# Writing out the small unit loops and dropping the increments behind the waits in a fused convolution and attention kernel

## The reference

```python
# layer 0: kernels turned by an angle that the input gives, grouped 3x3 convolution, gate
rot = vmap(vmap(_rotate_one, (None, 0)))(base_kernel, angles)
feat = conv(x, rot, feature_group_count=B * G)
return feat * sigmoid(relu(pooled @ meta_w1.T + meta_b1) @ meta_w2.T + meta_b2)
# layer 1: focused linear attention
q = (relu(q) + 1e-06) / scale ; k = (relu(k) + 1e-06) / scale
q = q**3 / norm(q**3) * norm(q) ; k = k**3 / norm(k**3) * norm(k)
kv_state = einsum('bjc,bjd->bcd', k, v)
z = 1.0 / (einsum('bic,bc->bi', q, k.sum(axis=1)) + 1e-06)
out = einsum('bic,bcd->bid', q, kv_state) * z
out = out + depthwise_5x5(v)
return out @ Wproj.T + bproj
# together
x = x + layer0(group_norm(x)) ; x = x + layer1(group_norm(x))
```

## Time and profile before

| | us |
|---|---|
| median of 3 timed executions | 3786.84 |
| lowest, highest | 3786.37, 3790.71 |
| profiled execution | 3783.43 |
| its span in the trace | 3781.6 |

### The profile page before, as it was taken

The page is one execution under the profiler, slowest core; times in us unless marked ns, Lnnn a source line. Parts: engine busy times, 40 slices in busy tenths (PEclk is TensorE's granted clock), DMA queues, the critical chain, the costliest instruction groups (busy, mean ns, idle before and its releaser), DMA issues.

```text
span 3781.6 us, 84370 instructions
## 1 busy us (share of the span) xinstructions
PE 3485.4 (92%) x27988; PEld 2840.5 (75%) x27988; DVE 2762.7 (73%) x6715; ACT 2658.7 (70%) x7096; POOL 1606.0 (42%) x1557
## 2 busy tenths in 40 slices
PE   1669999999999999999999999999999999999897
PEld 1238787877878778787877878787787878778786
DVE  7776876767787676777767677776767777575747
ACT  2347777777777777777867777776777777676775
POOL 5542553625345262544626254462625436250402
PEclk9889999999999999999999999999999999999999
DMA  6662634536354453635445363544626343360402
GB/s 222 207 194 68 188 114 143 156 108 190 104 171 118 142 170 97 192 113 161 122 141 176 92 191 120 150 130 124 196 80 192 118 148 113 109 181 1 119 6 79
DMA packets 559906, 515.10 MB, mean 136 GB/s; under 512 B 97600, under 2 KB 491968, under 8 KB 559552
## 3 DMA queue, kind: packets, MB, share of 16 engines
q1 hardware_dynamic: 555200, 508.99, 44.7%
q10 hardware_dynamic: 4352, 1.57, 0.2%
HBM read 351.06 MB, written 134.22 MB: 128 GB/s over the span
## 4 chain that ended last, share of the span: by engine, by line
PE 76%; DVE 10%; ACT 8%; issue 4%; DMA 1%; SPq 1%; POOL 0%; DVEq 0%; ACTq 0%; POOLq 0%
PE SM L1524 15%; PE F L1541 15%; PE VAB L1541 8%; PE PP L1632 7%; PE F L1580 6%; PE VAB L1580 6%; PE T L1552 5%; PE VAB L1610 5%; PE T L1601 3%; PE F L1543 2%; ACT K L1308 2%; PE T L1620 2%; PE VAB L1543 1%; DVE F L996 1%; DVE XR L1068 1%
## 5 line engine op out<-in xcount | busy, mean ns | idle before, releaser
L1541 PE MATMUL F<-WQ,XHL 128*128 128x256 f16 x6144 | 812.7, 273 | 15.9 <-ACT V L1345 15.9
L661 POOL TENSOR_TENSOR XR<-XR,V 128x512 f32<-128x512 f32 x256 | 325.8, 1273 | 904.3 <-DVE XR L1057 904.3
L1314 ACT ACTIVATE K<-K,SCAL 128x256 f32<-128x256 f32 x1024 | 514.0, 509 | 225.4 <-DVE K L1002 224.6
L636 POOL TENSOR_TENSOR SL<-PL,SL 128x1122 f16<-128x1122 f32 x112 | 259.9, 2320 | 970.5 <-DVE SL L970 970.5
L1541 PEld LDWEIGHTS F<-WQ,XHL 128*128 128x128 f16 (+1 forms) x6144 | 599.9, 98 | 89.6 <-issue 19.8
L1524 PE MATMUL SM<-SL,BD 128*128 128x512 f16 x2688 | 634.9, 385 | 0.0
L1308 ACT ACTIVATE K<-F,SCAL 128x256 f32<-128x256 f32 x1024 | 474.8, 469 | 215.3 <-DVE F L996 213.3
L1002 DVE TENSOR_TENSOR K<-K,F 128x512 f32<-128x512 f32 x512 | 350.4, 684 | 228.8 <-PE T L1552 112.3
L1524 PEld LDWEIGHTS SM<-SL,BD 128*128 128x128 f16 x2688 | 260.9, 97 | 284.2
L996 DVE TENSOR_TENSOR F<-F,FL 128x512 f32<-128x512 f32 x512 | 353.5, 690 | 144.5 <-PE F L1543 139.5
L1632 PE MATMUL PP<-XR,WP 128*128 128x256 f16 x3072 | 380.6, 274 | 46.1 <-DVE XR L1075 46.1
(11 more groups left out here) (202 smaller groups left out, 6864.1 us busy)
## 6 DMA issues: line engine op xcount, KB each, us to landing
XR<-xr SPq DMA_DIRECT2D x132, 512.0 KB, 5.0
U<-x SPq DMA_DIRECT2D x256, 256.0 KB, 3.4
XR<-x SPq DMA_DIRECT2D x256, 256.0 KB, 4.1
out<-XR SPq DMA_DIRECT2D x256, 256.0 KB, 3.4
PL<-xp SPq DMA_DIRECT2D x112, 561.0 KB, 3.8
RX<-xr SPq DMA_DIRECT2D x118, 512.0 KB, 3.8
x<-RX SPq DMA_DIRECT2D x448, 128.0 KB, 2.8
BD<-RX SPq DMA_DIRECT2D x240, 96.0 KB, 2.2
```

Source lines behind the costliest of these rows:

```text
L661: g_.tensor_tensor(o, o, fm, ALU.add).then_inc(o_rdy, 2)
L1314: a.activation(K2[:, p, t * C:(t + 1) * C], K3[:, p, t * C:(t + 1) * C], ACT.Square, scale=inv_a, accum_out=S6[:, 2 * p + t:2 * p + t + 1] ...
L1541: t_.matmul(o, XHL[:, xa, h, at], WQ[:, wa, h, c0:c0 + C], start=(k == 0), stop=False)
```

## The change

All `carry(...)` calls, the function and the semaphore go. A wait that had one is then taken up by the operation that follows it: with one wait the operation itself waits; with several, the first one written goes onto the operation and the later ones onto event instructions ahead of it. The loops on VectorE, TensorE and ScalarE become Python loops, so that their rounds are written out with constants. Instructions in the program, before and after: TensorE 24781 and 27612, VectorE 8362 and 8665, ScalarE 4095 and 5633, GpSimd 3209 and 2112, SyncE 2995 and 2007. No computing instruction changes its place among the others on any engine. The lines of the new program are 35 to 45 lower (L1308 is L1266, L1541 is L1499, L661 is L623).

The core of the diff:

```diff
-        carried = sem("carried")
...
-        def carry(eng):
-            eng.sem_inc(carried, 1)
...
                 ins.then_inc(rot_chain, 1)
                 pool.wait_ge(rot_chain, c * N_ROT + steps[0])
-                carry(pool)
...
             def add_depthwise(b, u, p):
                 m = b * PAIRS + 2 * u + p
                 pool.wait_ge(z_rdy, 4 * m + 4 + Z_CR)
-                carry(pool)
...
             def batch(b, ahead):
                 s1, s2, s3 = ahead >= 1, ahead >= 2, ahead >= 3
                 low_v(b, 0, 0)
-                with dve.Fori(1, 5) as u:
+                for u in range(1, 5):
                     for p in range(2):
                         step_kv(b, u, p)
...
-                with act.Fori(1, NU) as u:
+                for u in range(1, NU):
                     for p in range(2):
                         step_kv(b, u, p)
...
                 pe.wait_ge(ones_rdy, b + 1)
-                carry(pe)
-                with pe.Fori(1, 5) as u:
+                for u in range(1, 5):
                     for p in range(2):
                         step_kv(b, u, p)
...
                 pe.wait_ge(fm_rdy, HD * (b + 1) + FM_CR)
-                carry(pe)
                 pe.wait_ge(state_rdy, 4 * HPH * (b + 1))
                 if s2:
 
                     if s3:
                         pe.wait_ge(zb_rdy, b + 4)
                     pe.wait_ge(root_rdy, b + 5)
                     pe.wait_ge(wt_in, 256 * (b + 3))
-                    carry(pe)
```

More of the change, by code:

```diff
@@ L346, in load_taps @@
                     sp.wait_ge(tp_rdy, i - 2)
-                    carry(sp)
                 sp.dma_start(taps_tile(i), toeplitz[:, i * PIX:(i + 1) * PIX]).then_inc(taps_in[i % 3], 16)
@@ L858, in deviations @@
                 dve.wait_ge(s0_rdy, pixels)
-                carry(dve)
                 if not early(k):
                     dve.wait_ge(s1_rdy, results)
-                    carry(dve)
                 for layer in range(2):
```

## The result

| | before | after |
|---|---|---|
| median | 3787.49 us (4 runs, 3786.37 to 3790.71) | 3919.03 us (4 runs, 3918.45 to 3920.87) |
| ratio, with 95% interval | | 1.0348 [1.0335, 1.0361] |
| span of the profiled execution | 3781.6 us | 3917.3 us |

The account below looks back on a forecast made before the run. TensorE, busy 92% of the span, was taken to bound the kernel, with VectorE at 73%. Terms of -2, -1.3, -1.8, -3.9, -0.9 and -0.6 summed to -10.5 us, from 3786.84 to 3776.3, range 3765 to 3790.

Parts of the forecast that it names:

- What bounds the kernel: Whole kernel: TensorE busy 92%, VectorE 73%; only setup, batch 14's query phase and a handful of gaps can be shortened.
- Part 1, the loops: Writing out loops: -0.6 us at TensorE's loop entry, -1.3 from ScalarE's loop at the key/value phase's end.
- rival D: TensorE's 64 loop jumps all count because they break instruction flow: another 13.8 us won, 3762.5; chance 0.04.
- Part 2: Removing increments from waits: -3.9 and -1.8 us through GpSimd's L661, -0.9 at TensorE's events, -2 in setup.
- The price of the link: GpSimd's start behind its releaser: 0.18 us falls to 0.05, so -0.13 a link, bounds 0 and -0.16.
- The -3.9 us for batches 14 and 15: Query steps there: L661 starts 0.13 us earlier and releases VectorE's held L1009 sooner, 0.13 x 30.
- The -1.8 us for the convolving phases: One L1009 stall on the chain in each of 14 convolving batches shortens by 0.13 us, 0.13 x 14.
- TensorE's three events: Events ahead of the first query projection (gap 1.01 us) lose increments: 0.3 us in the last three batches, -0.9.
- The setup: Setup chain's carried waits on SyncE, VectorE and GpSimd get cheaper: -2 us, bounds 0 and -3.8.
- A: Rival: GpSimd wakes no sooner, 0.18 us being its wake-up price; both L661 terms go, 3782.7; chance 0.19.
- B: Rival: GpSimd's closed-up links starve VectorE in the key/value phase, +21 us over the other terms, 3797; chance 0.11.
- C: Rival: shifted gaps change TensorE's six 1.2 GHz stretches to none (-9) or twelve (+9); chance 0.05 longer, 0.04 shorter.

Follow-up runs that it names:

- one_inc_gone: The kernel before the change without one increment, that of conv_low's wait on GpSimd: 3878.00 us, ratio 1.0241.
- one_inc_back: The changed kernel with one increment put back, behind conv_low's wait on GpSimd (128 executions): 3814.94 us, ratio 1.0073 to before.
- before_scalar: The kernel before the change with the product in `ratio` as two one-column products by a per-partition scalar: 3782.05 us, ratio 0.9988.
- link_incs_back: The changed kernel with only the increments of link put back, between GpSimd's 27 kernel-rotation operations: 3886.17 us, ratio 1.0261 to before.

## Why the prediction was wrong, step by step

**What bounds the kernel** held: TensorE, with VectorE close behind. What I didn't price is how little VectorE had to spare in the query phases: 98 us of 129 by average, but 2.14 us more on every second step shows up as 0.6 to 1.2 us of TensorE's waiting.

**Part 1, the loops**, had sign and mechanism right. Forecast -1.9, measured -4.9 by the medians; 0.28 us a key/value phase, 14 x 0.28 = 3.9, where 0.12 a batch were taken. The gap before the last L1552 fell from 0.90 to 0.81, as the prediction said; where the other 0.19 us lie wasn't looked into. All the rounds of three engines together are worth 3.8 to 10.6 us, so the 13.8 that rival D adds for TensorE's jumps alone are excluded.

**Part 2** is where it failed, at the sentence "Where does a link of GpSimd stand on the path? Most don't: it is busy 42%". I looked for links whose result somebody waits for, and found L661. I didn't ask whom each operation overtakes when it starts 0.1 us sooner. The rows for it were at hand: the earlier trace rows show the product held for up to 1.25 us, why, and the same two engines meet behind every cast, 0.07 us apart, in a part of the trace I had read only for L661. The sum has no term for that meeting: it stood at nothing, and it cost 92 us by `one_inc_gone` and 104 by `one_inc_back`. The earlier start was a gain in the one place and the trigger of a 2.3 us stall in the other.

The price of the link was mis-sized as well. Taken: -0.13 everywhere. Measured: the depthwise addition starts 0.143 us behind its quotient instead of 0.180 (medians of 256), so -0.04; the subtraction 0.079 instead of 0.180, so -0.10; the rotation's links 0.08 instead of 0.18, so -0.10. The trace after shows why the first of these is smaller. The text ahead of the prediction says that L623 waits itself after the change; in the trace an event instruction for its wait (L620) still stands ahead of every one, and only the increment is gone:

```profile
L620 POOLq EVENT_SEMAPHORE  x256: 17/17/43, 383.5 to 3904.8; - x128
L600 POOLq EVENT_SEMAPHORE  x19: 17/17/17, 107.8 to 3394.6; - x19
```

The 14 subtractions right behind an event of L600 start 0.144 us behind their cast, the 98 others 0.079. So on GpSimd the price was 0.18 us with event and increment, 0.14 with the event alone and 0.08 where the operation waits itself. The -3.9 us for batches 14 and 15 shrink with it: a step went from 5.68 to 5.64 us there, and the product from 0.70 to 0.67. The mechanism of that term was right. The two query phases are 0.9 us longer each in the profile after nevertheless, and other runs scatter by as much. The -1.8 us for the convolving phases can't be seen beside the 107.

**TensorE's three events** did what was said: the gap ahead of the first query projection fell from 1.01 to 0.66 us, and the next wait (L1559, for VectorE's cube) rose from 0.21 to 0.54. The kernel after:

```profile
1067.55 0.83 PE L1499 MATMUL F<-WQ,XHL 128*128 128x256 f16 x6 [0.66 <-ACT V L1303]
1073.98 0.66 PE L1559 MATMUL T<-MATS,K 128*128 128x128 f32 x4 [0.54 <-DVE K L960]
```

**The setup** was to win 2 us and is 4.2 longer in the profile. In `before_scalar`, which touches next to nothing there, it is 268.3 us against 265.6 before, so a few microseconds of the setup come and go from run to run, and the term can't be judged.

**The rivals.** A: GpSimd does wake sooner, in part. A's own reason, that the wake-up belongs to the engine, holds for the 0.08 us that stay even where the operation waits itself. B is the mechanism that came, and its sign: GpSimd, with its links closed up, holding VectorE. But I had put it into the key/value phase alone, at +21 us, and gave it 0.11. There it cost 16.5 with the clock's share in it, which `link_incs_back` takes away again, and it fell on the product of `ratio` more than on the L1014 that I had named; the same contest in the query phase cost 107. My argument against it ("the burst gets shorter, so the stalls end earlier") counted GpSimd's time and not who is first. C came too: by the granted clock in the trace TensorE ran at 1.2 GHz in 18 stretches, against six, eight of them behind the gaps of 1.44 and 0.81 us at the end of a key/value phase, which are no longer than before. At the 1.5 us a stretch of the prediction that is 12 x 1.5 = 18 us of the 131, spread over the phases; the link increments put back remove most of them. It isn't luck, since the five profiles with the longer key/value phases have 14 to 18 such stretches and the nine others 4 to 8, but what in those phases brings them isn't shown. I had named twelve, +9, as the far end. One such group in the kernel after, 2.09 us instead of 1.16:

```profile
566.96 2.09 PE L1510 MATMUL T<-VT,K 128*128 128x129 f32 x8 [0.81 <-DVE K L972]
```

## What to carry to other kernels

An instruction that computes nothing may be holding an engine back at the right moment; before it is removed, list for VectorE and GpSimd not only who waits for the earlier result but what each operation will now start ahead of, above all where one releases the other and both go on. A tiny VectorE operation with two tensors right behind a release of GpSimd is such a place: a margin of 0.07 us decided over 92 to 104 us. The robust cure is neither a delay nor luck but an operation that isn't held, or one that is through before the release.

## What the runs showed of the hardware

- VectorE's product of two columns, 0.16 us alone, took 2.30 us when GpSimd's operation had begun 0.02 to 0.03 us before it, and 0.16 when it began 0.04 to 0.08 us before GpSimd's.
- Two products of one column by a scalar, 0.33 us together, were not held (GpSimd first by 0.02 us); two of 256 columns were, 1.65 us instead of 0.61. Their free time a column is half of that of a product of two tensors.
- GpSimd's operation starts 0.18 us behind the operation that releases it when an event instruction with an increment stands between, 0.14 when the event has no increment, and 0.08 when the operation waits itself.
